# A decoder layer on one core: routing and weight splits reordered at the passage to the experts

## Chip, cores and metric

One Trainium2 chip, one of its cores. The metric is the device time of one launch in microseconds. Five engines work side by side, each through its own queue in order: TensorE (PE), VectorE (DVE), ScalarE (ACT), GpSimd (POOL) and SyncE (SP), which only issues DMAs here. They wait for one another through semaphores.

## What is computed

`x` is (32, 112, 256) in float32, the context (32, 375, 256). Cut to its three residual steps the reference is:

```python
x = x + attn(layernorm(x))          # one head over the features, softmax, projection, residual inside
x = x + xattn(layernorm(x), ctx)    # similarity, c2q and q2c attention, four blocks through W_l (z)
x = x + ffn(layernorm(x))           # below
# ffn: 3584 tokens, 8 experts of 256 -> 128 -> 256 and one shared expert
scores = sigmoid(x @ gate_w.T); scores_c = scores + correction_bias
# 4 groups of 2 experts: the best 2 groups by the sum of scores_c; in them the best 4 experts by scores_c
# their scores divided by their sum, times 2.5: cw (tokens x 8)
y = einsum(silu(x @ Wg[e]) * (x @ Wu[e]) @ Wd[e], cw) + shared_mlp(x)
```

Every product that matters is made of three matmuls in a fast float32 form: both operands are split in a high part (a rounded copy, made by ScalarE) and a low part (the rest, a subtraction made by VectorE or GpSimd), and `mm3` (L75 to L77) adds high x low, low x high and high x high.

## The kernel before

**Two blocks.** The first block takes the 32 sequences in 8 groups of 4 through both attentions. The second takes the 3584 tokens in 7 groups of 512 (`g` = 0 to 6) through the experts. Between the blocks all engines meet; nothing of the second block starts before every engine has ended the first.

**The last attention group does expert work ahead.** There the first block already normalises, transposes and routes expert group 0, normalises group 1, splits the weights of experts 0, 1 (`w01_low`, GpSimd) and 2 (`w2_lo`, GpSimd), and runs gate and up products of the shared expert and of experts 0 and 1 (`gate_up_early`). In VectorE's queue the order is: the row statistics and `sinv2`; `route_groups` (11 small steps, each waiting for the one before); the reduction `mneg`; `normalise3(1)`; the low parts and products of c2q (`x_low`, `x3_product`, `x3_low`) with `mrow` between; `route_experts` (12 steps, the last writes `cw`); `af[0]`; the q2c sums, the `wz` sums with their low parts; two x2 sums with `op_lo0` between; `af[1]`. GpSimd does there `c_lo`, four adds to `x2b`, `w01_low(1)`, `w2_lo`, and the weighting of `sg[1]` by `cw`. TensorE transposes `cw` (`turn_cw`) behind the shared expert's gate and up.

**An expert group in the second block.** `ORDER` puts the shared expert at n = 0 and experts 0 to 7 at n = 1 to 8. For each n the engines do:
- TensorE: gate and up (12 matmuls of 512 columns), then the down product of n - 2 (12 of 256 columns). Behind that, at n = 1 it transposes the next group's rows, at n = 2 it makes its routing logits, at n = 3 it turns them, at n = 6 it turns the next group's `cw` (`turn_cw`, L224), which waits for the 23rd routing step.
- ScalarE: silu of the gate (L1544), at n = 6 the copy of `cw`, then the high part of the product (L1548).
- GpSimd: the silu times the spread `cw` (L1586), for n of 1 and above.
- VectorE: up times the weighted silu (`product`, L1610), then its low part (`act_low`, L1615). Behind n = 3 it adds the logits and does `route_groups`, behind n = 4 `route_experts`.

Gate and up of n wait for `product(n - 2)`, whose end frees their banks. In group 0 everything of the routing is one expert later (`late`), and the weights of the experts at n = 4 to 8 are split there: the high part on ScalarE (L1539) and the low on VectorE (L1627) at n = 2 to 6, one at each. GpSimd's weighting and the product of n = 1 in group 0 lie at the end of the first block.

**The end.** `finish` adds the down products of a group to x2 in two halves behind `y_mm`, one count per group, and `store` sends 512 KB in one DMA.

Of the kernel before, what the change touches and what calls it, by code (L numbers as in the profile page):

```python
# [26 lines left out]
ALU = mybir.AluOpType  # L27
# [23 lines left out]
def decoder_layer(nc, x, ctx, ctx_t, norm_w, norm_b, qkv_wt, qk_b, v_b, proj_wt, proj_b, w_cq, b_cq, w_c, b_c,  # L51
# [28 lines left out]
    with outer:  # L80
# [194 lines left out]
            step(dve.tensor_tensor(choice[:, :, :].rearrange("p t (a b) -> p t a b", b=2), halves,  # L275
                                   gmask[:, :, :].unsqueeze(3).to_broadcast([P, T, 4, 2]), ALU.mult))

        def route_experts(dve, g):

            step = stepper(dve, g, 11)  # L280

            mine, other = pairs(choice[:, :, :], 8, 3), pairs(choice[:, :, :], 8, 2)
            step(dve.tensor_tensor(e_gt[:, :, :, :], other, mine, ALU.is_gt))  # L283
            step(dve.tensor_tensor(e_eq[:, :, :, :], other, mine, ALU.is_equal))  # L284
            step(dve.tensor_tensor(e_eq[:, :, :, :], e_eq[:, :, :, :], tri8[:, :, :].unsqueeze(1).to_broadcast([P, T, 8, 8]), ALU.mult))  # L285
            step(dve.tensor_tensor(e_gt[:, :, :, :], e_gt[:, :, :, :], e_eq[:, :, :, :], ALU.add))  # L286
            step(dve.reduce_sum(erank[:, :, :], e_gt[:, :, :, :], AX))  # L287
            step(dve.tensor_scalar(erank[:, :, :], erank[:, :, :], 4.0, None, ALU.is_lt))
            step(dve.tensor_tensor(wsel[:, :, :], score[:, :, :], erank[:, :, :], ALU.mult))
            step(dve.reduce_sum(wsum[:, :], wsel[:, :, :], AX))  # L290
            step(dve.tensor_scalar(wsum[:, :], wsum[:, :], ROUTE_TINY, None, ALU.add))
            step(dve.reciprocal(winv[:, :], wsum[:, :]))
            step(dve.tensor_tensor(wsel[:, :, :], wsel[:, :, :], winv[:, :].unsqueeze(2).to_broadcast([P, T, NEXP]), ALU.mult))
            step(dve.tensor_scalar(cw[:, :, :], wsel[:, :, :], EXPERT_SCALE, None, ALU.mult))


        with ExitStack() as c1:
# [204 lines left out]
            def _(pe):  # L502
# [44 lines left out]
                def group(i, last_group):  # L547
# [192 lines left out]
                    if last_group:  # L740
                        pe.wait_ge(shared_lo_ok, 1)
                        pe.wait_ge(x3_ok, ev[G - 1])
                        gate_up_early(0, shared_hi[:, 0:GU + D], shared_lo[:, 0:GU + D])
                        turn_cw(pe, 0, h_bank[1])
                        pe.wait_ge(w01_lo_ok, 1)
                        gate_up_early(1, wqkv_hi[:, 0, :], wqkv_lo[:, 0, :])
                        pe.wait_ge(af_ok, 1)
                        pe.wait_ge(w01_lo_ok, 2)
                        gate_up_early(0, wqkv_hi[:, 1, :], wqkv_lo[:, 1, :])
                        pe.wait_ge(cwt_ok, 1)  # L750
                        pe.wait_ge(cb_ok, i + 1)
                        turn_h3(pe, 1)
                        for j in range(G):
                            z_c(i, j)
# [8 lines left out]
            def _(act):  # L763
# [24 lines left out]
                def group(i, last):  # L788
# [147 lines left out]
                    if last:  # L936
                        act.activation(silu_warm[:, :], mhalf2[:, 0:1], ACT.Silu)
                        act.wait_ge(wx_in[DONE], 48)
                        act.activation(w2_hi[:, :], w_staged[0][:, :], ACT.Copy).then_inc(e_hi_ok, 1)
                        act.wait_ge(gu_mm, 1)  # L940
                        act.activation(sg[0][:, :], bank[0][:, :], ACT.Silu).then_inc(sg_ok, 1)
                        act.wait_ge(af_ok, 1)
                        act.activation(op_hi0[:, :], af[0][:, :], ACT.Copy).then_inc(a_hi_ok, 1)
                        copy_cw(act, 0, h_bank[1])
                        act.wait_ge(gu_mm, 3)
                        act.activation(sg[1][:, :], bank[1][:, :], ACT.Silu).then_inc(sg_ok, 1)
                        for j in range(G):
                            wz_high(i, j)
                    else:
                        residual(i + 1)  # L950
                        h_high_pair(i + 1, 1)
# [14 lines left out]
            def _(pool):  # L966
# [37 lines left out]
                def group(i, last):  # L1004
# [34 lines left out]
                    pool.tensor_tensor(c_lo[:, :, :, :], ct[:, :, :, :], f32(c_hi[:, :, :, :]), ALU.subtract).then_inc(c_lo_ok, 1)  # L1039
                    if is_first(i):  # L1040
                        pool.wait_ge(late_in, 16 * LATE_LOADS)
                    for j in range(G):
                        pool.wait_ge(c_ok, ev[j])
                        if j == 0:
                            pool.wait_ge(x2_st, 16 * (i + 1))
                        pool.tensor_tensor(x2b[:, j, :], x1[:, j, :], bl_wide[:, :], ALU.add).then_inc(x1b_ok, 1)
                    if last:
                        w01_low(1)
                        pool.wait_ge(e_hi_ok, 1)
                        pool.tensor_tensor(w2_lo[:, :], w_staged[0][:, :], f32(w2_hi[:, :]), ALU.subtract).then_inc(e_lo_ok, 1)  # L1050
                        pool.wait_ge(sg_ok, 2)
                        pool.wait_ge(cw_in, 16)
                        pool.tensor_tensor(sg[1][:, :], sg[1][:, :], cw_wide0[:, 0, :], ALU.mult).then_inc(sgw_ok, 1)

                pool.wait_ge(consts, 4)
                ln1_scalars(0)
# [6 lines left out]
            def _(dve):  # L1063
# [39 lines left out]
                def group(i, last):  # L1103
# [186 lines left out]
                    dve.wait_ge(exp2_ok, ev[G - 1])  # L1290
                    dve.reciprocal(sinv2[:, :], ssum2[:, :]).then_inc(sinv2_ok, G)
                    if last:
                        route_groups(dve, 0)
                    dve.wait_ge(t_m, i + 1)
                    dve.reduce_max(mneg[:, :], m_bank[0:G, 0:L], AX, negate=True).then_inc(mneg_ok, 1)
                    if last:
                        normalise3(dve, 1)
                    else:
                        normalise_h(i + 1)
                    x_low(0)  # L1300
                    x3_product(0)
# [16 lines left out]
                    if not last:  # L1318
                        h_low_pair(i + 1, 1)
                    if last:  # L1320
                        route_experts(dve, 0)
                        dve.wait_ge(gu_mm, 2)
                        dve.wait_ge(sg_ok, 1)
                        dve.tensor_tensor(af[0][:, :], bank[2][:, :], sg[0][:, :], ALU.mult).then_inc(af_ok, 1)
# [8 lines left out]
                    if not last:  # L1333
                        for j in range(G):
                            wz_sum(j)
                    else:
                        wz_sum(0)
                        wz_sum(1)
                        wz_low_last(0)
                        wz_sum(2)  # L1340
                        wz_low_last(1)
                        wz_sum(3)
                        wz_low_last(2)
                        wz_low_last(3)
                        x2_sum(i, 0)
                        dve.wait_ge(a_hi_ok, 1)
                        dve.tensor_tensor(op_lo0[:, :], af[0][:, :], f32(op_hi0[:, :]), ALU.subtract).then_inc(a_lo_ok, 1)
                        x2_sum(i, 1)
                        dve.wait_ge(gu_mm, 4)
                        dve.wait_ge(sgw_ok, 1)  # L1350
                        dve.tensor_tensor(af[1][:, :], bank[3][:, :], sg[1][:, :], ALU.mult).then_inc(af_ok, 1)

                dve.memset(mhalf[:, :], -0.5).then_inc(consts, 1)
                dve.memset(eps[:, :], LN_EPS).then_inc(consts, 1)
# [38 lines left out]
        with ExitStack() as c2:  # L1393
# [5 lines left out]

            g_bank, u_bank, y_bank = bank[0:2], bank[2:4], bank[4:6]  # L1400
            AHEAD = 2


            w_f = [None] * DONE + w_staged + [sb(f"w_f{e}", [P, GU + D]) for e in range(DONE + STAGED, NEXP)]
# [19 lines left out]
            def _(sp):  # L1424
# [47 lines left out]
                    group(2 * it + 2, 0, True)  # L1472
                group(NG2 - 2, 1, False)
                store(NG2 - 2, 1)
                store(NG2 - 1, 0)
                sp.wait_ge(out_st, 16 * NG2)

            @block.tensor
            def _(pe):
# [12 lines left out]
                def down(g, n):  # L1492
# [4 lines left out]
                    for t in range(T):  # L1497
                        s = slice(t * P, (t + 1) * P)
                        last = mm3(pe, y_bank[t // 2][:, (t % 2) * D:(t % 2 + 1) * D], a_hi[b][:, s], a_lo[b][:, s], w_hi[e][:, GU:GU + D],
                                   w_lo[e][:, GU:GU + D], n == 0 and t % 2 == 0, n == NE - 1, skip_group_check=True)  # L1500
                    if n == NE - 1:
                        last.then_inc(y_mm, 1)

                def group(g, p, last):
                    late = 1 if is_first(g) else 0
# [29 lines left out]
            def _(act):  # L1535
# [14 lines left out]
                def group(g, p, last):  # L1550
                    late = 1 if is_first(g) else 0
                    for n in range(NE):
                        if not is_first(g) or n >= DONE:
                            expert(g, p, n)
                        if is_first(g) and 1 < n and n + 2 < NE:
                            split_high(n + 2)
                        if not last:
                            if n == 1:
                                h3_high(act, g + 1, h3_hi[1 - p])
# [18 lines left out]
            def _(pool):  # L1578
# [9 lines left out]
                def group(g, p, last):  # L1588
                    if not last and not is_first(g):
                        rstd3(pool, g + 1)  # L1590
                    for n in range(2 if is_first(g) else 1, NE):
                        expert(g, p, n)

                group(0, 0, False)
# [7 lines left out]
            def _(dve):  # L1602
# [12 lines left out]
                    dve.tensor_tensor(a_lo[b][:, :], af[(p + n) % 2][:, :], f32(a_hi[b][:, :]), ALU.subtract).then_inc(a_lo_ok, 1)  # L1615

                def finish(g, p, nth):
                    dve.wait_ge(y_mm, g + 1)
                    dve.wait_ge(x2_in[p], 16 * nth)
                    for q in range(2):  # L1620
                        x2q = x2t[p][:, 2 * q:2 * q + 2, :]
                        dve.tensor_tensor(x2q, y_bank[q][:, :].rearrange("p (t d) -> p t d", t=2), x2q, ALU.add).then_inc(out_ok, 1)

# [5 lines left out]
                def group(g, p, nth, last):  # L1629
# [1 line left out]
                        moments3(dve, g + 1)  # L1631
                    late = 1 if is_first(g) else 0
                    for n in range(NE):
                        if not is_first(g) or n >= DONE:
                            product(g, p, n)
                        if is_first(g) and 1 < n and n + 2 < NE:
                            split_low(n + 2)
                        if n == 1 and not is_first(g):
                            finish(g - 1, 1 - p, nth)
                        if not last:  # L1640
# [7 lines left out]
                            sum_logits(dve, g + 1)  # L1648
                            route_groups(dve, g + 1)
                        if n == 4 + late and not last:  # L1650
                            route_experts(dve, g + 1)

                group(0, 0, None, False)
                with dve.Fori(0, NG2 // 2 - 1) as it:
# [40 lines left out]
```

## Time and profile before

| what | value |
|---|---|
| three runs | 682.79, 685.2, 685.92 us (median 685.2) |
| the profiled execution | 681.68 us |
| its span, first to last instruction | 679.9 us |
| busy: TensorE, VectorE, ScalarE, GpSimd | 96%, 71%, 50%, 37% of the span |

A line of the timeline has the start and the length in us, the engine, the line of the kernel, the operation, what it writes and reads, the shape, and in brackets the idle time before it with what ended that. A matmul's end is modelled, and matmuls overlap; so TensorE's pace is read from start to start.

### The profile page before, as it was taken

How to read it: one execution, taken by the hardware profiler on the slowest of the kernel's cores; microseconds unless marked ns; L12 is line 12 of the kernel's file. 1: busy time of each engine (PE TensorE's matmuls, PEld its weight loads, DVE VectorE, ACT ScalarE, POOL GpSimd, SP SyncE). 2: the span in 40 equal slices, each digit the busy share in tenths (PEclk: the TensorE clock that was granted, in tenths of full speed). 3: DMA queues.
4: the chain of work that ended last, by engine and by line, in shares of the span. 5: the costliest groups of instructions: out<-in, count | busy, mean ns of one | idle time of the engine just before them, and what ended most of it. 6: DMA issues, size and time to landing. Idle time of an engine off the chain costs nothing. (4 is left out here: it accounts for less than half of the span.)

```text
span 679.9 us, 11725 instructions
## 1 busy us (share of the span) xinstructions
PE 652.6 (96%) x3848; PEld 553.3 (81%) x3848; DVE 484.8 (71%) x1262; ACT 341.7 (50%) x794; POOL 249.2 (37%) x322
## 2 busy tenths in 40 slices
PE   3999999999999999999999889999999999999997
PEld 2868878888788788887886777888888888888886
DVE  4678778778787787777888978765767656577433
ACT  4655675666556656665576445343423334233321
POOL 2145365172452642724652422322233232322331
PEclk9999999999999999999999999999999999999999
DMA  7625134043150340522633080423212132310300
GB/s 211 161 52 149 39 98 139 0 130 104 51 156 28 105 130 0 152 83 55 196 89 105 27 272 10 143 76 125 93 62 99 58 124 93 121 66 2 145 11 32
DMA packets 51774, 64.44 MB, mean 95 GB/s; under 512 B 3912, under 2 KB 49528, under 8 KB 50848
## 3 DMA queue, kind: packets, MB, share of 16 engines
q1 hardware_dynamic: 51744, 64.06, 30.5%
q8 instruction: 16, 0.26, 0.2%
q14 instruction: 14, 0.11, 0.1%
HBM read 56.60 MB, written 7.45 MB: 94 GB/s over the span
## 5 line engine op out<-in xcount | busy, mean ns | idle before, releaser
L1586 POOL TENSOR_TENSOR xt<-xt,cw_wide 128x512 f32<-128x512 f32 x55 | 72.1, 1311 | 177.3 <-ACT xt L1544 177.3
L1610 DVE TENSOR_TENSOR res<-bank,xt 128x512 f32<-128x512 f32 x61 | 41.9, 687 | 56.9 <-POOL xt L1586 52.5
L1548 ACT ACTIVATE a_hi<-res 128x512 fp32r<-128x512 f32 x42 | 26.6, 634 | 98.7 <-DVE res L1610 98.7
L75 PE MATMUL bank<-h_hi,w_lo 128*128 128x512 f32 x168 | 67.4, 401 | 1.8 <-DVE w_lo L1627 1.1
L76 PE MATMUL bank<-h_lo,w_hi 128*128 128x512 f32 x168 | 66.1, 393 | 0.0
L77 PE MATMUL bank<-h_hi,w_hi 128*128 128x512 f32 x168 | 66.0, 393 | 0.0
L75 PE MATMUL bank<-w_hi,op_lo 128*128 128x256 f32 x184 | 55.3, 300 | 1.1 <-DVE op_lo L1124 0.6
L76 PE MATMUL bank<-w_lo,op_hi 128*128 128x256 f32 x184 | 51.4, 279 | 0.0
L77 PE MATMUL bank<-w_hi,op_hi 128*128 128x256 f32 x184 | 51.3, 279 | 0.0
L1615 DVE TENSOR_TENSOR a_lo<-res,a_hi 128x512 fp32r<-128x512 f32 x42 | 33.6, 799 | 22.4 <-ACT a_hi L1548 22.4
L1002 POOL TENSOR_TENSOR wz_lo<-tmp,wz_hi 128x512 fp32r<-128x512 f32 x28 | 35.1, 1283 | 37.6 <-DVE tmp L1167 37.6
L631 PE MATMUL bank<-ctxf,qg 125*112 125x256 f32 x192 | 46.7, 379 | 0.0
L618 PE MATMUL bank<-cw_wide,ctw 128*112 128x375 f32 x128 | 46.3, 483 | 0.1
L1544 ACT ACTIVATE xt<-bank 128x512 f32<-128x512 f32 x61 | 36.0, 591 | 12.6 <-PE bank L77 12.1
L75 PE MATMUL bank<-wl_hi,op_lo 128*112 128x256 f32 x128 | 38.2, 298 | 2.5 <-DVE op_lo L1146 1.3
L795 ACT ACTIVATE bank<-bank,smx 128x256 f32<-128x256 f32 x64 | 28.8, 454 | 22.6 <-DVE smx L1114 22.6
L75 PEld LDWEIGHTS bank<-h_hi,w_lo 128*128 128x128 f32 x168 | 31.5, 188 | 10.1 <-DVE res L1610 3.5
L75 PEld LDWEIGHTS bank<-w_hi,op_lo 128*128 128x128 f32 x184 | 34.5, 188 | 6.0 <-DVE op_lo L1124 4.1
L1124 DVE SCALAR_TENSOR_TENSOR op_lo<-bank,sinv,op_hi 128x256 fp32r<-128x256 f32 x64 | 28.0, 478 | 15.5 <-ACT op_hi L803 14.8
L1020 POOL TENSOR_TENSOR r2a<-mv,eps 112x1 f32<-112x1 f32 x32 | 6.1, 191 | 89.7 <-DVE mv L1137 89.7
L77 PEld LDWEIGHTS bank<-h_hi,w_hi 128*128 128x128 f32 x168 | 31.5, 188 | 7.4
L76 PEld LDWEIGHTS bank<-h_lo,w_hi 128*128 128x128 f32 x168 | 31.6, 188 | 5.8
(240 smaller groups left out, 2041.4 us busy)
## 6 DMA issues: line engine op xcount, KB each, us to landing
cw_wide<-in_ctx_t SPq DMA_DIRECT2D x32, 375.0 KB
ctxf<-in_ctx SPq DMA_DIRECT2D x32, 375.0 KB
cw_wide<-cw_scratch SPq DMA_DIRECT2D x7, 1536.0 KB, 7.6
xt<-in_x SPq DMA_DIRECT2D x8, 448.0 KB, 4.0
x_scratch<-x2b SPq DMA_DIRECT2D x8, 448.0 KB, 3.3
x2n<-x_scratch SPq DMA_DIRECT2D x7, 512.0 KB, 4.7
cw_wide<-cw_scratch SPq DMA_DIRECT2D x7, 512.0 KB, 4.3
x2t<-x_scratch SPq DMA_DIRECT2D x7, 512.0 KB, 4.0
```

What stands on the lines that cost most here:

```text
L75: pe.matmul(dst, a_lo, b_hi, start=first, stop=False, **kw)
L76: pe.matmul(dst, a_hi, b_lo, start=False, stop=False, **kw)
L77: return pe.matmul(dst, a_hi, b_hi, start=False, stop=last, **kw)
L618: last = pe.matmul(bank[j][0:L, 0:S], ctw[:, j, k, :], ctxtf[:, j, k, :], start=(k == 0), stop=(k == KB - 1))
L631: last = pe.matmul(bank[j][0:L, 0:D], at[j][:, b * L:(b + 1) * L], ctxf[0:SB, j, b, :], start=(b == 0), stop=(b == NSB - 1))
L795: e = act.activation(bank[j][:, n], bank[j][:, n], ACT.Exp, bias=smx[:, j, half:half + 1], accum_out=ssum[:, j, half:half + 1])
L1002: pool.tensor_tensor(wz_lo[:, j, :, :], wz[:, j, :, :], f32(wz_hi[:, j, :, :]), ALU.subtract).then_inc(wz_lo_ok, 1)
L1124: w = dve.scalar_tensor_tensor(op_lo[j][:, n], bank[j][:, n], sinv[:, j, half:half + 1], f32(op_hi[j][:, n]), ALU.mult, ALU.subtract)
L1544: act.activation(sg[b][:, :], g_bank[b][:, :], ACT.Silu).then_inc(sg_ok, 1)
L1586: pool.tensor_tensor(sg[b][:, :], sg[b][:, :], cw_wide[p][:, ORDER[n], :], ALU.mult).then_inc(sgw_ok, 1)
L1610: dve.tensor_tensor(af[b][:, :], u_bank[b][:, :], sg[b][:, :], ALU.mult).then_inc(af_ok, 1)
L1615: dve.tensor_tensor(a_lo[b][:, :], af[(p + n) % 2][:, :], f32(a_hi[b][:, :]), ALU.subtract).then_inc(a_lo_ok, 1)
```

## The change

Seven edits, in the order of the diff:
- `route_experts` is cut in two: `route_ranks` (4 steps) and `route_weights` (8 steps). In the expert loop the ranks stay behind n = 4 and the weights go behind n = 5 (both one later in group 0).
- In the last attention group `turn_cw` goes behind `gate_up_early` of expert 0 on TensorE, and `copy_cw` behind the second silu on ScalarE.
- GpSimd does `w01_low(1)` ahead of the `x2b` adds and waits for the whole routing before them. `w2_lo` goes to VectorE, between the x2 sums. The weighting of `sg[1]` and `af[1]` leave the first block; the second block's loops take n = 1 of group 0 in.
- On VectorE `normalise3(1)` goes ahead of `mneg`, and the whole routing goes behind the low parts.
- The splits of group 0 follow a list: two at n = 2, then one each at n = 3, 4 and 5.
- `y_mm` counts each half of a group's down product, and `finish` waits for each half.
- The last group is stored in two halves.

```diff
-        def route_experts(dve, g):
+        def route_ranks(dve, g):
             step = stepper(dve, g, 11)
...
             step(dve.tensor_tensor(e_gt[:, :, :, :], e_gt[:, :, :, :], e_eq[:, :, :, :], ALU.add))
+
+        def route_weights(dve, g):
+
+            step = stepper(dve, g, 15)
             step(dve.reduce_sum(erank[:, :, :], e_gt[:, :, :, :], AX))
...
                         gate_up_early(0, shared_hi[:, 0:GU + D], shared_lo[:, 0:GU + D])
-                        turn_cw(pe, 0, h_bank[1])
                         pe.wait_ge(w01_lo_ok, 1)
                         gate_up_early(1, wqkv_hi[:, 0, :], wqkv_lo[:, 0, :])
+                        turn_cw(pe, 0, h_bank[1])
...
-                        copy_cw(act, 0, h_bank[1])
                         act.wait_ge(gu_mm, 3)
                         act.activation(sg[1][:, :], bank[1][:, :], ACT.Silu).then_inc(sg_ok, 1)
+                        copy_cw(act, 0, h_bank[1])
...
+                    if last:
+                        w01_low(1)
+                        pool.wait_ge(route, ROUTE_STEPS)
                     for j in range(G):
...
-                    if last:
-                        w01_low(1)
-                        pool.wait_ge(e_hi_ok, 1)
-                        pool.tensor_tensor(w2_lo[:, :], w_staged[0][:, :], f32(w2_hi[:, :]), ALU.subtract).then_inc(e_lo_ok, 1)
-                        pool.wait_ge(sg_ok, 2)
-                        pool.wait_ge(cw_in, 16)
-                        pool.tensor_tensor(sg[1][:, :], sg[1][:, :], cw_wide0[:, 0, :], ALU.mult).then_inc(sgw_ok, 1)
...
                     if last:
-                        route_groups(dve, 0)
+                        normalise3(dve, 1)
                     dve.wait_ge(t_m, i + 1)
...
-                    if last:
-                        normalise3(dve, 1)
-                    else:
+                    if not last:
                         normalise_h(i + 1)
...
                     if last:
-                        route_experts(dve, 0)
+                        route_groups(dve, 0)
+                        route_ranks(dve, 0)
+                        route_weights(dve, 0)
...
+                        dve.wait_ge(e_hi_ok, 1)
+                        dve.tensor_tensor(w2_lo[:, :], w_staged[0][:, :], f32(w2_hi[:, :]), ALU.subtract).then_inc(e_lo_ok, 1)
                         x2_sum(i, 1)
-                        dve.wait_ge(gu_mm, 4)
-                        dve.wait_ge(sgw_ok, 1)
-                        dve.tensor_tensor(af[1][:, :], bank[3][:, :], sg[1][:, :], ALU.mult).then_inc(af_ok, 1)
...
+            SPLITS = [(), (), (4, 5), (6,), (7,), (8,), (), (), ()]
...
-                store(NG2 - 1, 0)
-                sp.wait_ge(out_st, 16 * NG2)
+                for q in range(2):
+                    sp.wait_ge(out_ok, 2 * (NG2 - 1) + q + 1)
+                    n = slice(T * (NG2 - 1) + 2 * q, T * (NG2 - 1) + 2 * q + 2)
+                    sp.dma_start(out_g[:, n, :], x2t[0][:, 2 * q:2 * q + 2, :]).then_inc(out_st, 16)
+                sp.wait_ge(out_st, 16 * (NG2 + 1))
...
-                    if n == NE - 1:
-                        last.then_inc(y_mm, 1)
+                        if n == NE - 1 and t % 2:
+                            last.then_inc(y_mm, 1)
...
-                        if is_first(g) and 1 < n and n + 2 < NE:
-                            split_low(n + 2)
+                        if is_first(g):
+                            for m in SPLITS[n]:
+                                split_low(m)
...
                         if n == 4 + late and not last:
-                            route_experts(dve, g + 1)
+                            route_ranks(dve, g + 1)
+                        if n == 5 + late and not last:
+                            route_weights(dve, g + 1)
```

## Rows read from the trace of the kernel before

**Rows 1.** The page: busy us (share) xinstructions; granted TensorE clock in 40 slices.
```profile
PE 652.6 (96%) x3848; PEld 553.3 (81%) x3848; DVE 484.8 (71%) x1262; ACT 341.7 (50%) x794; POOL 249.2 (37%) x322
...
PEclk9999999999999999999999999999999999999999
```

**Rows 2.** Waits of TensorE: line, released by, us in total, times, longest.
```profile
PE bank L224 <- DVE cw L294: 1.3, 2, 1.1
...
PE bank L75 <- DVE op_lo L1146: 1.3, 1, 1.3
PE bank L75 <- DVE op_lo L1156: 1.2, 1, 1.2
```

**Rows 3.** Timeline of TensorE, first expert group, start and length in us.
```profile
398.51 0.35 PE L75 MATMUL bank<-shared_hi,op_lo 128*128 128x256 f32 x1 [1.73 <-PEq L297]
...
422.94 0.60 PE L224 MATMUL bank<-ident,cw 128*8 128x128 f32 x4 [0.20 <-DVE cw L294]
424.62 0.47 PE L75 MATMUL bank<-h_hi,w_lo 128*128 128x512 f32 x1 [1.08 <-DVE w_lo L1627]
```

**Rows 4.** Timeline of VectorE, one steady expert group.
```profile
491.20 0.18 DVE L263 TENSOR_SCALAR den<-den 128x32 f32<-128x32 f32 x1 [0.49 <-ACT den L229]
...
493.28 0.22 DVE L273 TENSOR_REDUCE grank<-g_gt 128x16 f32<-128x64 f32 x1
493.53 0.95 DVE L274 TENSOR_SCALAR gmask<-grank 128x16 f32<-128x16 f32 x1
...
494.93 0.69 DVE L1610 TENSOR_TENSOR res<-bank,xt 128x512 f32<-128x512 f32 x1 [0.22 <-DVE choice L275]
496.32 0.69 DVE L1615 TENSOR_TENSOR a_lo<-res,a_hi 128x512 fp32r<-128x512 f32 x1 [0.70 <-ACT a_hi L1548]
496.93 1.51 DVE L283 TENSOR_TENSOR e_gt<-choice 128x256 f32<-128x256 f32 x1
...
499.86 0.42 DVE L287 TENSOR_REDUCE erank<-e_gt 128x32 f32<-128x256 f32 x1
500.31 0.18 DVE L288 TENSOR_SCALAR erank<-erank 128x32 f32<-128x32 f32 x1
...
501.63 0.18 DVE L294 TENSOR_SCALAR cw<-wsel 128x32 f32<-128x32 f32 x1
```

**Rows 5.** Timeline of TensorE, the same group.
```profile
502.07 0.60 PE L224 MATMUL bank<-ident,cw 128*8 128x128 f32 x4
502.77 0.50 PE L75 MATMUL bank<-h_hi,w_lo 128*128 128x512 f32 x1
```

**Rows 6.** Timeline of ScalarE and of GpSimd, the same group.
```profile
495.66 0.63 ACT L1548 ACTIVATE a_hi<-res 128x512 fp32r<-128x512 f32 x1 [2.57 <-DVE res L1610]
496.20 0.58 ACT L1544 ACTIVATE xt<-bank 128x512 f32<-128x512 f32 x1
...
493.16 1.30 POOL L1586 TENSOR_TENSOR xt<-xt,cw_wide 128x512 f32<-128x512 f32 x1 [4.92 <-ACT xt L1544]
496.86 1.31 POOL L1586 TENSOR_TENSOR xt<-xt,cw_wide 128x512 f32<-128x512 f32 x1 [2.40 <-ACT xt L1544]
```

**Rows 7.** Timeline of VectorE, the passage.
```profile
373.93 1.38 DVE L1306 TENSOR_SCALAR mrow<-mexp,minv 4x112 f32<-4x112 f32 x1
...
375.54 2.14 DVE L1156 TENSOR_TENSOR op_lo<-tmp,op_hi 128x224 fp32r<-128x224 f32 x1
...
378.20 0.37 DVE L1156 TENSOR_TENSOR op_lo<-tmp,op_hi 128x224 fp32r<-128x224 f32 x1
...
393.37 2.39 DVE L1172 TENSOR_TENSOR wz_lo<-tmp,wz_hi 128x512 fp32r<-128x512 f32 x2
...
402.87 0.95 DVE L1627 TENSOR_TENSOR w_lo<-ctxf,w_hi 128x768 fp32r<-128x768 f32 x1
```

**Rows 8.** The end: VectorE's last adds; the last DMA, KB and us to landing.
```profile
675.26 1.29 DVE L1622 TENSOR_TENSOR x2t<-bank,x2t 128x512 f32<-128x512 f32 x2 [1.78 <-PE bank L77]
...
out_dram<-x2t SPq DMA_DIRECT2D x1, 512.0 KB, 2.9
```

More of the change, by code:

```diff
@@ L1554, in group @@
                             expert(g, p, n)
-                        if is_first(g) and 1 < n and n + 2 < NE:
-                            split_high(n + 2)
+                        if is_first(g):
+                            for m in SPLITS[n]:
+                                split_high(m)
                         if not last:
@@ L1590, in group @@
                         rstd3(pool, g + 1)
-                    for n in range(2 if is_first(g) else 1, NE):
+                    for n in range(1, NE):
                         expert(g, p, n)
@@ L1617, in finish @@
                 def finish(g, p, nth):
-                    dve.wait_ge(y_mm, g + 1)
                     dve.wait_ge(x2_in[p], 16 * nth)
                     for q in range(2):
+                        dve.wait_ge(y_mm, 2 * g + q + 1)
                         x2q = x2t[p][:, 2 * q:2 * q + 2, :]
@@ L1633, in group @@
                     for n in range(NE):
-                        if not is_first(g) or n >= DONE:
+                        if not is_first(g) or n >= 1:
                             product(g, p, n)
-                        if is_first(g) and 1 < n and n + 2 < NE:
-                            split_low(n + 2)
+                        if is_first(g):
+                            for m in SPLITS[n]:
+                                split_low(m)
                         if n == 1 and not is_first(g):
```

## The prediction

> **What bounds the kernel now.** I read the page's busy times first: TensorE is busy for 96% of the span [rows 1]. A change helps only where TensorE waits, and hurts wherever it makes TensorE wait anew. So I read next who TensorE waits for. Leaving the start aside, the larger waits lie in the passage from the last attention group to the first expert group (370 to 425 us): two of 1.3 and 1.2 us for low parts made by VectorE, 1.3 us in two pieces for the routing weights `cw` [rows 2], 1.73 us at the boundary of the two blocks, and 1.08 us for `product(6)` and a weight split [rows 3]. These are what the passage edits can win: about 6.6 us.
>
> Third I read one steady expert group in order of time, on every engine, because the diff edits the loop body too. There VectorE finishes `cw` at 501.63 + 0.18 = 501.81 us [rows 4] and TensorE starts the transpose of `cw` at 502.07 [rows 5]. TensorE arrives when the weights are 0.26 us old. The next gate matmuls begin at 502.77, and they wait for a product that is queued behind the routing. There are five steady groups that route (groups 1 to 5), all of this pattern, and the first expert group has it one expert later. This is the place that decides.
>
> **The lock that prices VectorE's queue.** GpSimd's product runs 493.16 to 494.46 [rows 6]. In that time VectorE's reduction of 493.28 takes 0.22 us, but its tensor_scalar of 493.53, of 16 columns, takes 0.95 and ends as GpSimd ends; a tensor_tensor with both inputs in SBUF (L283) takes 1.51, while the three like it that follow take 1.4 together (499.86 less 498.44), and again it ends as GpSimd's product of 496.86 ends [rows 4, 6]. So such a VectorE instruction issued while GpSimd works waits for GpSimd's end; a reduction does not.
>
> **Part 1: the routing in two pieces, in the five steady groups.** `route_experts` (12 steps behind `act_low(4)`) becomes `route_ranks` (4 steps, same place) and `route_weights` (8 steps behind `act_low(5)`). TensorE's `turn_cw` and ScalarE's `copy_cw` stay at expert 6. The ranks end where L287 starts now, 499.83. Then VectorE's queue holds `product(5)`, `act_low(5)`, and only then the weights:
> - `product(5)` starts 0.22 later, as the product behind the group steps does, at 500.05.
> - From a product's start to its low part's start is 496.32 - 494.93 = 1.39 [rows 4]: `act_low(5)` at 501.44, the weights at 502.05.
> - ScalarE's high part starts 0.73 after the product, its next silu 0.54 after that, GpSimd 0.66 after that [rows 4, 6]: GpSimd's product for expert 6 runs from 501.98 to 503.29, on top of the weights.
> - The reduction (L287) passes, 0.45. L288 is a tensor_scalar and waits until 503.31. From its end to the end of `cw` is 501.81 - 500.49 = 1.32 [rows 4]. So `cw` is ready at 504.63, 2.82 later than now.
> - TensorE, in order, stands at `turn_cw` from 502.07. `turn_cw` to the next gate matmul takes 0.36 without another wait (an estimate from 0.60 for its four transposes less their overlap with the next): the gate starts at 504.63 + 0.05 (the step from `cw` to L224) + 0.36 = 505.04 instead of 502.77.
>
> That is +2.27 us a group; the wait for the product that disappears is already inside it. Nothing hides it: behind `turn_cw` stand gate_up 7 and all that follows, and no engine has work that TensorE could take instead. Bounds: if GpSimd's lock does not meet the weights, `cw` is at 503.85 and the cost is 1.5; if the lock takes the reduction too, 2.7. I take 2.3, since L274 and L273 show the two behaviours. Times five: **+11.5** (7.5 to 13.5).
>
> **Part 2: the passage, up to the block boundary.** Moving `route_groups` behind the low parts lets `normalise3(1)` run 2.7 earlier (the 11 group steps are 491.20 to about 494.71 less the 0.77 of lock, [rows 4]), and so GpSimd's `c_lo` starts near 370.2. GpSimd then does `w01_low(1)` and waits for the 23rd routing step before the four `x2b` adds. Now the low parts lose time to GpSimd: L1306 takes 1.38 for 112 columns and an L1156 takes 2.14 instead of 0.37 [rows 7]. After, only L1306 still meets GpSimd (`w01_low(1)`, until about 374.1, where it ends at 375.31 now), and the x3 low parts run free. TensorE's waits of 1.3 and 1.2 go [rows 2] and it leaves the z products about 2.5 earlier. `turn_cw` moves behind gate_up 0 and arrives near 385.1. The routing now starts near 377.2 and takes 2.74 + 3.80 = 6.54 (its steps in [rows 4] less their lock time), `cw` at 383.8: covered by 1.3 us of TensorE's work. The four `x2b` adds wait for it and are done by 388 even at 1 us each; VectorE's x2 sums, the first to need them, come after 392.
>
> VectorE now starts its expert part 2.3 earlier. Then: the L1172 pair takes 2.39 [rows 7] where two of this shape (0.69 for L1615, [rows 4]) take 1.3; the rest is GpSimd's weighting, which goes: -1.1. `w2_lo` comes to VectorE: +0.87 (L1627 is the same shape, 0.95 with 0.08 of overlap). The product `af[1]` (L1351, the shape of L1610, 0.69, [rows 4]) leaves for the next block: -0.6. Sum: 2.3 + 1.1 - 0.9 + 0.6 = 3.1; I take the boundary at **-3.0** (395.5 instead of 398.51, [rows 3]). Bounds: -1.0, if the lock time only moves to other instructions, and -3.6, TensorE's own.
>
> **Part 3: the first expert group gives it back.** What left block 1 stands at the head of block 2, where nothing runs ahead: GpSimd's weighting of expert 1 (1.31 to 1.4) and then `product(1)`, and TensorE waits for the latter before gate_up 3 (0.6). VectorE is then 1.6 ahead of now. Two splits instead of one at n = 2 cost it another 0.87 [rows 7], and they also delay ScalarE's copy of the logits, for which TensorE waits about 1.1. VectorE is 0.75 ahead at `product(4)`; from there to `cw` its queue is as now, one split an expert, except for `product(6)`, `act_low(6)` and the lock: +2.82 as in part 1. `cw`, now just before 422.94, comes at 422.89 - 0.75 + 2.82 = 424.96. The last split is done by then, so gate_up 8 follows at 425.4, against 424.62 [rows 3]: **+0.8** for passage and first group together. Bounds: +1.3 with the reduction locked too, -3.0 if TensorE alone set the pace.
>
> **Part 4: the last store.** Two adds take 1.29, and the store of 512 KB lands 2.9 after its issue [rows 8]. After, the first add lies under TensorE's last two quarters of the product, and the second half's store is issued one add (0.6) earlier with half the bytes. Gain between 0.6 and 0.6 + 1.45; I take **-1.3**. By the Trainium skill (DMA: Bandwidth & Descriptors, Anatomy of one DMA) about 2 us of a DMA is fixed; by that, only half of the remaining 0.9 would be saved and this term would be -1.05, which no run here shows yet.
>
> `finish` waits for two counts per group instead of one; it runs with its product ready, so I cost it at nothing; if that cover were gone, 0.6 a group. SP's queue loses no place: the copy of `cw` goes out 2 to 3 us later and is needed at expert 1 of the next group, some 20 us on.
>
> **Sum.** +11.5 + 0.8 - 1.3 = +11.0 us. The profiled execution took 681.7 (span 679.9 and 1.8 around it): 692.7. The three runs shown are 1.1 to 4.2 above it; their median is 685.2, and the mean of all four is 683.9. I predict 683.9 + 11.0 = **694.9**.
>
> **Rivals.**
> - The lock misses the weights: ScalarE's silu for expert 6 comes later or earlier than I put it. Then 7.5 + 0 - 1.3 = +6.2: 690. The silu's place behind the high part speaks against.
> - Faster: `cw` is still in time. It decides at TensorE's arrival at `turn_cw` (502.07, [rows 5]): if the weights end before that, the split only takes the product out from behind the routing. Then each steady group wins 502.77 - 502.43 = 0.34, the first group keeps -3.0, the store -1.3: -6.0, 678. It would need `product(5)` and `act_low(5)` to cost nothing; they take 2.0 there [rows 4].
> - No difference: the passage keeps its 3.0 and the steady cost is at its low end less a part, 7.5 - 3.0 - 1.3 = +3.2: 687.
> - TensorE's clock falls. The page grants it 90% or more, of its two levels 2.4 GHz, in every slice of the passage too [rows 1], so the forecast adds nothing. But a stall of 2.6 (near 4 in the first group) is longer than the 1.73 of [rows 3]. If the twelve gate matmuls behind each of six such stalls ran at 1.2 GHz, each would cost its time again, 652.6/3848 = 0.17 us on average: 12 x 6 x 0.17 = +12 more, 707. The Trainium skill (TensorE: Matmul & The Clock Gate, Why this matters for your kernels) warns of just such gaps between bursts; the trace of before has none long enough to show it.
>
> **How the numbers follow.** Forecast 0.62, lock misses 0.15, no difference 0.08, faster 0.06, clock 0.09. The range leaves out the last two and most of "no difference": from the low ends (7.5, and -1 for the passage and store together, on the lowest run of 682.8: about 688) to the high ends (13.5 + 1.3 - 0.6 on 685.9: 700). A measurement can tell 0.5%, 3.4 us, from no change. Slower 0.86, same 0.08, faster 0.06.
>
> **What would show it.** TensorE's wait for `cw` at L224, now 1.3 us in all, becomes the largest of the kernel, near 2.5 us in each of five groups and over 3 in the first; each steady group grows by about 2.3; L288 takes about 1 us in each. The first matmul of block 2 moves from 398.51 to about 395.5, and gate_up 8 stays near 425. The last add ends one add nearer to the last matmul. I am wrong if L224 shows no wait, or if block 2 begins later than 397.

## The result, and the profile after

| | median | range | runs |
|---|---|---|---|
| before | 684.0 us | 681.38 to 685.92 | 4 |
| after | 702.08 us | 700.47 to 703.2 | 4 |

The ratio is 1.0275 (95%: 1.0253 to 1.0296): slower by 18.1 us, where 11.0 was forecast. The time lies above the range of 688 to 700. The profiled execution of after took 703.2 us with a span of 701.4, which is 21.5 more than the span before; the account of stretches below is of these two executions, and the 18.1 is of the medians.

The page of after; busy us (share) xinstructions, then the granted clock in 40 slices:

```profile
PE 664.0 (95%) x3848; PEld 561.7 (80%) x3848; DVE 476.1 (68%) x1263; ACT 343.4 (49%) x794; POOL 246.8 (35%) x321
...
PEclk9999999999999999999999999999999999999999
```

Against [rows 1] TensorE has as many instructions and is busy for 11.4 us more. A stall adds nothing to busy time, so some matmuls must have become longer, though the clock's row still shows 9 throughout. A slice is 17.5 us long and a 9 is only 90% or more: a few us at half clock fit into it unseen. The mean granted clock of the core does tell: 1.000 before, 0.985 after.

Waits of TensorE after (line, released by, us in total, times, longest), the two that the text needs:

```profile
PE bank L224 <- DVE cw L298: 15.4, 6, 3.1
...
PE bank L75 <- PEq L301: 2.5, 1, 2.5
```

The wait for `cw` was 1.3 us in two pieces [rows 2]; it is 15.4 in six, one for each group that routes the next one. The timeline of TensorE shows them, and the pace of the gate matmuls behind the third of the six stalls:

```profile
427.54 0.87 PE L224 MATMUL bank<-ident,cw 128*8 128x128 f32 x4 [3.09 <-DVE cw L298]
428.06 0.78 PE L75 MATMUL bank<-h_hi,w_lo 128*128 128x512 f32 x1
...
468.17 0.60 PE L224 MATMUL bank<-ident,cw 128*8 128x128 f32 x4 [2.65 <-DVE cw L298]
...
512.89 0.89 PE L224 MATMUL bank<-ident,cw 128*8 128x128 f32 x4 [2.42 <-DVE cw L298]
513.43 0.78 PE L75 MATMUL bank<-h_hi,w_lo 128*128 128x512 f32 x1
514.00 0.63 PE L76 MATMUL bank<-h_lo,w_hi 128*128 128x512 f32 x1
514.43 0.63 PE L77 MATMUL bank<-h_hi,w_hi 128*128 128x512 f32 x1
...
516.53 0.39 PE L76 MATMUL bank<-h_lo,w_hi 128*128 128x512 f32 x1
516.76 0.39 PE L77 MATMUL bank<-h_hi,w_hi 128*128 128x512 f32 x1
...
646.60 1.02 PE L224 MATMUL bank<-ident,cw 128*8 128x128 f32 x4 [2.30 <-DVE cw L298]
```

Behind the stall the matmuls of 512 columns start 0.43 apart, and from 516.53 on 0.23. The windows of the same stretch have the reason (stretch and its length in us; busy us of PE, PEld, DVE, ACT and POOL, each with its instructions; granted clock, DMA share, GB/s):

```profile
510.40:512.80 2.40, 0.08 (x1) 0.00 (x0) 2.16 (x8) 0.00 (x0) 1.09 (x1) 1.00 0.00 0
513.40:514.00 0.60, 0.60 (x3) 0.51 (x2) 0.35 (x1) 0.10 (x1) 0.00 (x0) 0.50 0.00 0
514.00:515.00 1.00, 1.00 (x4) 0.80 (x3) 0.00 (x0) 1.00 (x2) 0.00 (x0) 0.50 0.00 0
515.00:516.00 1.00, 1.00 (x4) 0.81 (x3) 0.69 (x1) 0.00 (x1) 0.00 (x0) 0.50 0.09 16
516.00:517.00 1.00, 1.00 (x5) 0.76 (x5) 0.00 (x0) 0.60 (x1) 0.00 (x0) 0.76 0.08 16
517.00:518.00 1.00, 1.00 (x7) 0.86 (x6) 0.00 (x0) 0.00 (x0) 0.95 (x1) 1.00 0.91 270
```

TensorE stands idle until 512.89, and right behind that its granted clock is 0.50, the lower of the two levels, until about 516.5; from 517 on it is 1.00 again. Each of the six stalls at L224 has such a stretch: the clock is at 0.50 for some 3.4 us from 427.7, 468.7, 513.1, 557.4, 601.8 and 646.2. In the last three it falls up to 0.5 us before the stall ends.

What made `cw` late stands in the timelines of VectorE and GpSimd, here of the group of [rows 4], which begins later in this kernel:

```profile
507.64 0.43 DVE L286 TENSOR_TENSOR e_gt<-e_gt,e_eq 128x256 f32<-128x256 f32 x1
508.29 0.69 DVE L1614 TENSOR_TENSOR res<-bank,xt 128x512 f32<-128x512 f32 x1 [0.22 <-DVE e_gt L286]
509.68 0.69 DVE L1619 TENSOR_TENSOR a_lo<-res,a_hi 128x512 fp32r<-128x512 f32 x1 [0.70 <-ACT a_hi L1551]
510.29 0.41 DVE L291 TENSOR_REDUCE erank<-e_gt 128x32 f32<-128x256 f32 x1
510.74 0.80 DVE L292 TENSOR_SCALAR erank<-erank 128x32 f32<-128x32 f32 x1
...
512.65 0.18 DVE L298 TENSOR_SCALAR cw<-wsel 128x32 f32<-128x32 f32 x1
...
510.21 1.28 POOL L1590 TENSOR_TENSOR xt<-xt,cw_wide 128x512 f32<-128x512 f32 x1 [3.81 <-ACT xt L1547]
```

Between the ranks (L286) and the weights stand `product(5)` and `act_low(5)`. The reduction (L291) passes beside GpSimd's product; L292, 0.18 before [rows 4], takes 0.80 and ends as GpSimd ends, 511.5. The Trainium skill (SBUF — State Buffer, Who interferes with whom) calls the ports that VectorE and GpSimd share an exclusive lock; L292's 0.80 agrees.

The passage is read from the m transpose of the last attention group to the first matmul of block 2 (first row: before; the others: after; TensorE):

```profile
368.89 0.26 PE L715 MATMUL bank<-ident,m 112*4 112x112 f32 x1
```
```profile
371.48 0.26 PE L719 MATMUL bank<-ident,m 112*4 112x112 f32 x1
...
398.46 0.36 PE L75 MATMUL bank<-shared_hi,op_lo 128*128 128x256 f32 x1 [2.49 <-PEq L301]
```

It takes 26.98 us, and took 29.62 (to 398.51, [rows 3]): 2.64 less. This run of after enters it 2.59 later than the run before did. Seven kernels below have the code of after up to there. Five of them (e1, e3, e4, e5, e7) enter it between 369.05 and 369.58, e8 at 370.24 and e6 at 370.78, so most of that shift is of this execution and not of the change.

At the end, VectorE's last adds, the store's issues, and the DMA's KB and us to landing:

```profile
697.36 1.34 DVE L1626 TENSOR_TENSOR x2t<-bank,x2t 128x512 f32<-128x512 f32 x2 [1.15 <-PE bank L77]
698.08 1.02 SPq L1478 DMA_DIRECT2D out_dram<-x2t  x2
...
out_dram<-x2t SPq DMA_DIRECT2D x2, 256.0 KB, 2.2
```

From start to start along TensorE the 21.5 us of the two spans add up:

| stretch | before | after | difference |
|---|---|---|---|
| start to the m transpose | 368.89 | 371.48 | +2.59 |
| to block 2's first matmul | 29.62 | 26.98 | -2.64 |
| to gate_up 8 of the first group | 26.11 | 29.60 | +3.49 |
| to L224 of the next group | 36.23 | 40.11 | +3.88 |
| four group periods, L224 to L224 | 164.19 | 178.43 | +14.24 |
| last L224 to the last matmul | 49.91 | 51.09 | +1.18 |
| to the end of the span | 4.95 | 3.71 | -1.24 |

The four periods before are read between these two transposes, those of after between 468.17 and 646.60 above:

```profile
460.85 0.60 PE L224 MATMUL bank<-ident,cw 128*8 128x128 f32 x4
...
625.04 0.60 PE L224 MATMUL bank<-ident,cw 128*8 128x128 f32 x4
```

A steady group costs 3.56 more, where 2.27 was forecast.

### The profile page after: what moved, and what is told of

It reads as the page before. It is cut to its first block and busy times, and to the rows that moved or that the text cites. A ratio compares the mean times of both kernels' runs of the same rounds, so it can differ in the third digit from the quotient of the medians.

```text
span 701.4 us, 11730 instructions
## 1 busy us (share of the span) xinstructions
PE 664.0 (95%) x3848; PEld 561.7 (80%) x3848; DVE 476.1 (68%) x1263; ACT 343.4 (49%) x794; POOL 246.8 (35%) x321
## 5 line engine op out<-in xcount | busy, mean ns | idle before, releaser
L1590 POOL TENSOR_TENSOR xt<-xt,cw_wide 128x512 f32<-128x512 f32 x56 | 73.9, 1320 | 204.4 <-ACT xt L1547 194.9
L75 PE MATMUL bank<-h_hi,w_lo 128*128 128x512 f32 x168 | 71.0, 423 | 0.5 <-DVE res L1614 0.5
L76 PE MATMUL bank<-h_lo,w_hi 128*128 128x512 f32 x168 | 69.1, 411 | 0.0
L77 PE MATMUL bank<-h_hi,w_hi 128*128 128x512 f32 x168 | 68.4, 407 | 0.0
L1619 DVE TENSOR_TENSOR a_lo<-res,a_hi 128x512 fp32r<-128x512 f32 x42 | 30.1, 716 | 23.1 <-ACT a_hi L1551 23.1
L75 PEld LDWEIGHTS bank<-h_hi,w_lo 128*128 128x128 f32 x168 | 33.8, 201 | 8.4 <-DVE res L1614 0.7
L77 PEld LDWEIGHTS bank<-h_hi,w_hi 128*128 128x128 f32 x168 | 33.4, 199 | 8.1
L76 PEld LDWEIGHTS bank<-h_lo,w_hi 128*128 128x128 f32 x168 | 33.6, 200 | 6.2
L1124 DVE SCALAR_TENSOR_TENSOR op_lo<-bank,sinv,op_hi 128x256 fp32r<-128x256 f32 x64 | 28.0, 479 | 15.4 <-ACT op_hi L807 14.8
```

The costliest lines, as they stand in the source:

```text
L75: pe.matmul(dst, a_lo, b_hi, start=first, stop=False, **kw)
L76: pe.matmul(dst, a_hi, b_lo, start=False, stop=False, **kw)
L77: return pe.matmul(dst, a_hi, b_hi, start=False, stop=last, **kw)
L1590: pool.tensor_tensor(sg[b][:, :], sg[b][:, :], cw_wide[p][:, ORDER[n], :], ALU.mult).then_inc(sgw_ok, 1)
```

## Experiments

Theory: the split makes TensorE wait at `turn_cw`, some 2.1 us a group, and what the forecast lacks (7 to 9 us) is the clock that falls behind each stall. Rivals: the stalls alone are dearer than the sum had them, through their consequences on other engines; or another part of the change loses time. Ratios are against the kernel before on the same chip, 683.46 us for e1 to e4 and 683.8 for e5 to e8, with 95% intervals.

**e1 and e2: the split undone, and the split alone.** e1 is after with the weights directly behind the ranks; e2 is before with the split as its only edit.

```diff
 e1, on after
-                        if n == 5 + late and not last:
                             route_weights(dve, g + 1)
 e2, on before
...
-                            route_experts(dve, g + 1)
+                            route_ranks(dve, g + 1)
+                        if n == 5 + late and not last:
+                            route_weights(dve, g + 1)
```

> The changed kernel with one edit undone: the weights follow the ranks at once, behind expert 4 (5 in group 0), in front of product(5). Theory A (the loss is six stalls of TensorE at L224 and the fall of its clock behind each): no wait for cw over 0.5 us in the steady groups, granted clock 1.00 throughout, and what is left are the passage (-2.6, read from 368.89 to 398.51 before against 371.48 to 398.46 after) and the last store (-0.7 to -1.3): about 680, ratio 0.993 to 0.996. Rival B (the passage edits and the new split list lose, the split of the routing is beside the point): above 690, with TensorE waiting in the first expert group.

> The kernel before with the split of the routing alone: weights behind expert 5 (6 in group 0), all else as before. Theory A: the six stalls and the six clock falls are all here, without the gains: about 684 + 6 x 3.5 = 705, ratio 1.028 to 1.034, L224 near 15 us of wait, clock 0.985. Rival B: within 3 us of 684, since it has none of the passage edits.

e1 took 681.35 us, ratio 0.9978 (0.996 to 0.9996). e2 took 703.37, ratio 1.0291 (1.0256 to 1.0325). The split alone brings the whole loss; the other edits together win a little, though less than the 0.993 to 0.996 that e1 was expected to reach. TensorE's waits in e2:

```profile
PE bank L224 <- DVE cw L298: 16.2, 7, 2.9
```

(Its seventh is 1.11 us in the passage.) In e2 the first group's stall of 2.86 was not followed by a lower clock; the five of 2.29 to 2.59 were. In e1, expected at full clock throughout, the wait at the boundary of the blocks was. Its first matmul of block 2 on TensorE, and the windows behind it:

```profile
396.33 0.36 PE L75 MATMUL bank<-shared_hi,op_lo 128*128 128x256 f32 x1 [2.48 <-PEq L301]
```
```profile
398.00:399.00 1.00, 0.61 (x2) 0.48 (x2) 1.00 (x3) 0.50 (x1) 0.00 (x0) 0.50 0.86 254
399.00:400.00 1.00, 1.00 (x4) 0.71 (x4) 1.00 (x3) 1.00 (x3) 0.30 (x1) 0.50 0.85 255
```

**e4: the stall filled.** After, with nine useless matmuls of 512 columns (twelve in group 0) ahead of `turn_cw`, so that TensorE works on while `cw` is made. `cw` comes no earlier; only the idle time is gone. This is the test between clock and stall.

```diff
                         if n == 6 + late and not last:
+                            e = ORDER[n]
+                            for r in range(12 if late else 9):
+                                pe.matmul(h_bank[1][:, :], gate_up_weights(w_hi[e])[:, 0, 0, :], h3_hi[p][:, 0, :], start=True, stop=True)
```

> The changed kernel with matmuls of no use in front of each transpose of cw in the loop (9 of 512 columns, 12 in group 0, into a bank that is free there): TensorE is busy for about 2.1 us (2.8) of the 2.5 us (3.1) for which it stood idle; the weights come no earlier. Theory A with the clock as its own cost (1.4 to 1.7 us behind each stall): the clock stays at 1.00 and 6 x 1.5 = 9 us come back, 693, ratio 1.012 to 1.016. Rival C (the low clock costs nothing, since the stall alone sets the pace): 702, no change against the changed kernel.

692.94 us, ratio 1.0146 (1.0113 to 1.0179). Waits, the first and the last transpose of the steady groups, and the windows of the second steady group, filled and behind:

```profile
PE bank L224 <- DVE cw L298: 2.4, 6, 0.6
```
```profile
464.48 0.60 PE L224 MATMUL bank<-ident,cw 128*8 128x128 f32 x4 [0.61 <-DVE cw L298]
...
637.13 0.60 PE L224 MATMUL bank<-ident,cw 128*8 128x128 f32 x4 [0.26 <-DVE cw L298]
```
```profile
505.00:507.40 2.40, 2.36 (x12) 1.59 (x10) 2.19 (x8) 0.00 (x0) 1.29 (x1) 1.00 0.00 0
508.00:509.00 1.00, 1.00 (x7) 0.85 (x5) 0.55 (x1) 0.59 (x2) 0.00 (x0) 1.00 0.00 0
509.00:510.00 1.00, 1.00 (x6) 0.78 (x6) 0.45 (x1) 0.79 (x2) 0.00 (x0) 1.00 0.08 14
```

The clock stays at 1.00 there; the one fall of this profile is at the boundary of the blocks, at 396.2. TensorE still waits a little for `cw` each time, so a group is as late as the stall alone makes it: its period is 43.16 us against 41.05 before, +2.1. Against before, after is 18.1 us slower and e4 9.5: work that computes nothing wins 8.6 us, and the intervals of the two ratios do not overlap. So the idle time itself cost that, through the clock.

**e5 and e6: shorter stalls.** e5 puts the weights ahead of `act_low(5)` (`act_low(6)` in group 0). e6 holds GpSimd's product of expert 6 (7 in group 0) until the routing is done, which takes the lock away from L292.

```diff
 e5, on after: these two lines, moved ahead of act_low
                         if n == 5 + late and not last:
                             route_weights(dve, g + 1)
 e6, on after: in GpSimd's loop
+                        if n == 6 + (1 if is_first(g) else 0) and not last:
+                            pool.wait_ge(route, ROUTE_STEPS * (g + 2))
```

> The changed kernel with the weights in front of act_low(5) instead of behind it (act_low(6) in group 0): the wait for ScalarE's high part and the low part, 1.99 us, no longer stand ahead of them, but GpSimd's product of expert 6 (501.98 to 503.29 on the clock of the rows before) then meets their last steps, of which the product with 1/sum has two SBUF inputs. If the lock is as read: cw at 503.5 to 503.7, a stall of 1.4 to 1.7 us instead of 2.55; without the lock 502.5 and a stall of 0.4. Theory A with the clock falling only behind the longer stalls: no fall, 684 - 3 + 6 x 1.2 = 688, ratio 1.004 to 1.010. If the clock falls behind 1.5 us too: 696.

> The changed kernel with GpSimd's product of expert 6 (7 in group 0) held back until the weights are done, so that its lock can't meet them: the step at L292 takes 0.18 us instead of 0.80, cw is 0.62 earlier, the stall 1.9 us instead of 2.5 (2.5 instead of 3.1 in group 0). product(6) comes later but gate_up 8, which waits for it, has 4 us of TensorE's work as cover. If the clock falls as before: 702 - 6 x 0.6 = 698.5, ratio 1.021. If it stays at 1.00 behind stalls of 1.9: 6 x 1.4 less, 690, ratio 1.009. If the lock costs nothing: 702.

e5: 687.76 us, ratio 1.0062 (1.0045 to 1.0079). e6: 691.22, ratio 1.0114 (1.0084 to 1.0144). From e5, TensorE's waits and VectorE's L297; from e6, the waits and L292:

```profile
PE bank L224 <- DVE cw L298: 9.3, 6, 2.0
...
505.21 1.09 DVE L297 TENSOR_TENSOR wsel<-wsel,winv 128x32 f32<-128x32 f32 x1
```
```profile
PE bank L224 <- DVE cw L298: 11.7, 6, 2.5
...
507.17 0.18 DVE L292 TENSOR_SCALAR erank<-erank 128x32 f32<-128x32 f32 x1
```

In e5 GpSimd's product now meets L297 instead: the lock moves to whichever step is there. In e6 L292 is back at 0.18, and the steady period is 42.51, +1.46: the forecast's lower bound of 1.5, "if GpSimd's lock does not meet the weights", is the case that this measures. On the clock: e6's stalls are 2.46, 2.00, 1.78, 1.97, 1.79 and 1.65, and only the first is followed by a fall. e5's are 1.99, 1.99 and four of 1.2 to 1.5, and only the second is. Stalls 0.6 us shorter on average (11.7 against 15.4 in six) made e6 lose 7.4 us against before where after loses 18.1.

**e3: the transpose later.** After, with `turn_cw` and `copy_cw` one expert later. The weights keep their late place, but TensorE comes to them when they are ready.

```diff
-                        if n == 6 + late and not last:
+                        if n == 7 + late and not last:
...
-                            if n == 6 + late:
+                            if n == 7 + late:
```

> The changed kernel with TensorE's transpose of cw and ScalarE's copy of it one expert later (n = 7, 8 in group 0): the split stays, the wait for cw gets 4.2 us of TensorE's work as cover. Theory A: cw is ready 2.5 us after TensorE's former arrival, so no wait at L224, clock 1.00, and also the 0.3 to 0.4 us that the kernel before waited behind its routing go: 678 to 680, ratio 0.990 to 0.995. Rival B: above 690.

677.91 us, ratio 0.9934 (0.9909 to 0.9958): faster than both kernels. No wait for `cw` is left at L224, here in a steady group, one expert later:

```profile
504.93 0.60 PE L224 MATMUL bank<-ident,cw 128*8 128x128 f32 x4
```

The mean granted clock is 0.999, and the steady period is 40.65, 0.40 under before. That is what the "faster" rival said of weights that are in time (0.34 a group, 678 in all); it only needed the transpose moved too.

**e7 and e8: the boundary of the blocks.** TensorE waits 2.5 us there in after, 1.73 before [rows 3]. VectorE's last instruction of block 1 is the second x2 sum, behind which SyncE still issues its DMA. e7 is e3 with that sum ahead of `w2_lo`. e8 is e7 with eight useless matmuls that TensorE runs while it would wait for the boundary.

```diff
 e7, on e3
+                        x2_sum(i, 1)
                         dve.wait_ge(e_hi_ok, 1)
                         dve.tensor_tensor(w2_lo[:, :], w_staged[0][:, :], f32(w2_hi[:, :]), ALU.subtract).then_inc(e_lo_ok, 1)
-                        x2_sum(i, 1)
 e8, on e7
+                        pe.wait_ge(sg_ok, 2)
+                        for r in range(8):
+                            pe.matmul(bank[1][:, :], gate_up_weights(wqkv_hi[:, 1, :])[:, 0, 0, :], h3_hi0[:, 0, :], start=True, stop=True)
```

> e3_turn_later with one edit more: the second x2 sum in front of w2_lo at the end of the first block, so that SyncE's store of x2 is issued while VectorE still works. The changed kernel's first matmul of block 2 comes 0.84 us after VectorE's last instruction, the kernel before's 0.33. If SyncE's issue is what the boundary waits for, 0.4 to 0.5 us come back and the gap of TensorE is 2.0 instead of 2.5: 677.4, too little for the clock of the runs but plain in the trace. If not, the gap stays at 2.5.

> e7_sum_first with 8 matmuls of no use at the end of TensorE's first block, 1.9 us into the gap at the boundary, into a bank that is free there. The same gap of 2.5 us was followed by a fall of the clock in e1_one_piece and e4_fill and by none in the changed kernel and e3_turn_later. Filled, no fall can follow: granted clock 1.00 behind it in the trace, and the runs spread less; median 677 to 678. If the matmuls delay the boundary, up to 1 us is lost.

e7: 677.59 us, ratio 0.9916 (0.9899 to 0.9932). e8: 677.61, ratio 0.9911 (0.9895 to 0.9928). Block 2's first matmul in e7 and in e8:

```profile
395.53 0.36 PE L75 MATMUL bank<-shared_hi,op_lo 128*128 128x256 f32 x1 [1.99 <-PEq L301]
```
```profile
396.87 0.36 PE L75 MATMUL bank<-shared_hi,op_lo 128*128 128x256 f32 x1 [0.30 <-PEq L301]
```

The wait is 0.5 shorter in e7, and its passage takes 26.48, also 0.5 less than after. In the times e7 and e3 can't be told apart. e8 takes the gap away but wins nothing over e7: at this gap e7's profile shows no fall that could be saved.

## Why the prediction was right and wrong

**The stall, right.** The place (L224), the cause (the weights behind `product(5)` and `act_low(5)`, with the lock on their tensor_scalar) and the size came out: five stalls forecast at 2.27 us a group, 2.1 measured in e4, where the clock stays up. L292 took 0.80, where the sum had 0.81 (from 502.50 to 503.31) and the sign to look for said about 1. e6 shows the lower bound with its condition. Over all groups, from gate_up 8 of the first to the last matmul, e4 takes 261.09 us and before 250.33: the late weights cost 10.8, where +11.5 was forecast.

**The clock, the step that failed.** The forecast said that it "adds nothing" for the clock, since the page grants 90% or more in every slice. That argued from a row of the kernel before, about a kernel with a gap that the old one doesn't have, and from slices too coarse to show one. The rival "TensorE's clock falls" is what happened, and it had a chance of 0.09. Its price was too high: +12, with six times twelve matmuls at half speed. Measured it is 8.6 by the medians of after and e4, each against before, and 8.5 in their profiles (269.63 less 261.09 us from gate_up 8 of the first group to the last matmul). That is about 1.4 us a fall: the lower level lasts some 3.4 us, not for all twelve matmuls, and in three of the six it begins while TensorE still stands idle. The forecast with the measured clock is 694.9 + 8.6 = 703.5, against 702.08. The Trainium skill (TensorE: Matmul & The Clock Gate, Why this matters for your kernels) warns against idle gaps between bursts of matmuls. The six stretches at 0.50 agree with that; but the gaps that it warns of are longer than most of these stalls, and here a stall of 2.30 us was enough.

The row could show no fall, and by luck: the profiled execution of before was one without any. Of the 22 executions of before that were timed beside the experiments, six have a mean granted clock of 1.000 and took 681.30 to 682.75 us; the other sixteen have 0.992 to 0.998 and took 683.05 to 685.09. So the clock falls in the kernel before too, and the forecast's base of 683.9 holds some of it. Where those falls lie is not known, as these executions left no trace.

**The passage, right in sum.** Forecast -3.0 to the boundary, measured -2.64. VectorE's last instruction ends 3.15 earlier, counted from the m transpose, where its sum had 3.1. What is missing is at the boundary itself: after, it opens 0.84 us behind VectorE's last instruction (the sum ends at 397.62), before 0.33 (398.18), and e7 gets 0.5 back by having SyncE's issue earlier. The first expert group gave back what was expected: gate_up 8 starts 0.85 later, counted from the m transpose, where the forecast had +0.8. The mark that block 2 should begin before 397 can't be read as an absolute time: 398.46 holds the 2.59 by which this execution entered the passage late, and in e1, e3 and e4 block 2 begins between 396.21 and 396.33.

**The store, right.** Forecast -1.3, measured -1.24. A half lands 2.2 us after its issue where the whole took 2.9 [rows 8], so half the bytes saved 0.7, the middle of the forecast's 0 to 1.45. The -1.05 that the prediction worked out from the Trainium skill (DMA: Bandwidth & Descriptors, Anatomy of one DMA) lies further off: by the two sizes about 1.5 us of such a store do not depend on its bytes (an estimate), not 2. That section is on DMAs that GpSimd issues; this store goes out on SyncE's queue.

**The range** left out the clock's rival on the ground of its small chance. Its own numbers spoke for more: it named stalls of 2.6 to 4 us where the longest of [rows 2, 3] was 1.73. Three smaller slips of the prediction did not decide. The lower end of the range, 682.8 with 7.5 and -1 for passage and store together, makes 689.3 and not 688. Without the lock `cw` comes at 504.00 by its rows, since L288 still takes its 0.18, so the lower bound of a group is 1.64 and not 1.5. And L283 of [rows 4] ends 0.27 us behind GpSimd's product, not with it.

## What to carry to other kernels

Splitting a chain on an engine that works in order moves its second piece behind whatever is queued between; look up when the consumer arrives, and move the consumer as well (e3: the same split, 24 us faster than after). Price a new TensorE stall as its length plus what the clock takes behind it, here 1.4 us for a stall of 2.3 to 3.1, and look at the granted clock in windows of 1 us, since 40 slices of a long kernel hide it. A stall that can't be removed can be filled with work of no use (e4: 8.6 us won).

## What the runs showed of the hardware

The fall is not a matter of the gap's length alone. Stalls at L224 of 2.29 to 3.09 were followed by a granted clock of 0.50 in 11 of 12 cases (after and e2), the exception being one of 2.86. Of the eleven stalls between 1.18 and 2.00 in e5 and e6, one was. The boundary's 2.5 us were followed by a fall in e1 and e4 and by none in after, e3, e5 and e6, with the same code ahead of it. In e2 one more fall, from 42.3 on, follows a wait of 2.73 us in the first block (L612, for `c`). What else decides was not settled by these runs. Nor does every fall cost the 1.4 us: e1's three executions at a mean clock of 1.000 (680.83 to 682.08) were no faster than its four at 0.997 (680.18 to 680.52), of which the profiled one has its fall at the boundary.

The lock was met by tensor_scalar and tensor_tensor instructions as small as 32 columns (L292 0.80, L297 1.09, both 0.18 to 0.19 when free), and not by the reduction L291 between (0.41 beside GpSimd's product and 0.41 in e6, where GpSimd rests).

One cause stays open: that of the start of the profiled run of after. There the matmuls of 512 columns stand 0.43 us apart until 21.5, where before they are 0.23 apart already at 16.9, with the same code in both; at the first group's m transpose after is 2.62 late (52.63 against 50.01), which is the 2.59 us of the account. The pace is that of the lower level, but the windows of both give 1.00 there: the granted clock of the profile doesn't show it.
